# Two chains of moments in one slot of a transformer kernel's first phase, merged into one

## The reference

```python
x = x + attn_a(layernorm(x))   # 16 heads of 8, rotary, full softmax over 256 keys
x = x + ffn(layernorm(x))      # token shift, sigmoid(xr W_r) * (relu(xk W_k)^2 W_v)
x = x + attn_b(layernorm(x))   # windowed attention, one gradient step of a small MLP, gates
x = x + ffn(layernorm(x))
```

```python
def _layernorm(x, axis=-1, eps=1e-05):
    m = jnp.mean(x, axis=axis, keepdims=True)
    v = jnp.var(x, axis=axis, keepdims=True)
    return (x - m) / jnp.sqrt(v + eps)
```

## Time and profile before

| | us |
|---|---|
| median of 3 runs | 1386.79 |
| profiled execution, time | 1383.6 |
| profiled execution, span of the trace | 1381.8 |

### The profile page before, as it was taken

The page is one execution under the profiler, slowest core; times in us unless marked ns, Lnnn a source line. Parts: engine busy times, 40 slices in busy tenths (PEclk is TensorE's granted clock), DMA queues, the critical chain, the costliest instruction groups (busy, mean ns, idle before and its releaser), DMA issues.

```text
span 1381.8 us, 33016 instructions
## 1 busy us (share of the span) xinstructions
PE 1302.5 (94%) x10579; PEld 859.7 (62%) x10579; DVE 1125.4 (81%) x2849; ACT 904.5 (65%) x2504; POOL 503.6 (36%) x815
## 2 busy tenths in 40 slices
PE   6889999999999999987899999999999998999996
PEld 5445555555555555544566666666666665888885
DVE  5888988888999988875788888888888875787876
ACT  3268888888888888875456556655665653656563
POOL 5536666666666666532111111111111100233232
PEclk9999999999999999999999999999999999999998
DMA  3323322222233322210100110010000001223230
GB/s 79 78 74 80 83 77 75 68 80 80 80 90 102 102 74 79 64 42 16 32 24 28 32 49 26 26 32 24 28 28 29 20 17 42 77 81 89 81 87 29
DMA packets 101964, 79.62 MB, mean 58 GB/s; under 512 B 13780, under 2 KB 95124, under 8 KB 101796
## 3 DMA queue, kind: packets, MB, share of 16 engines
q1 hardware_dynamic: 100820, 76.99, 20.2%
q10 hardware_dynamic: 976, 0.54, 0.2%
HBM read 49.70 MB, written 27.79 MB: 56 GB/s over the span
## 4 chain that ended last, share of the span: by engine, by line
PE 49%; DVE 1%; issue 1%; ACT 0%; POOL 0%; DMA 0%; POOLq 0%; SPq 0%; DVEq 0%; ACTq 0%
PE b_g L1383 4%; PE b_psZ L1399 4%; PE b_psD L1320 4%; PE b_g L1370 4%; PE b_psZ L1331 4%; PE d_psO L1939 4%; PE d_psH L1931 4%; PE b_psM L1432 2%; PE b_psR L1376 2%; PE b_psL L1361 2%; PE b_psR L1392 2%; PE b_psD L1422 2%; PE b_psM L1444 1%; PE b_psM L1452 1%; PE d_psG L1957 1%
## 5 line engine op out<-in xcount | busy, mean ns | idle before, releaser
L793 DVE TENSOR_REDUCE a_MX<-a_psS 128x4 f32<-128x1024 f32 x248 | 302.7, 1220 | 40.2 <-PE a_psS L304 40.2
L596 ACT ACTIVATE a_PT<-a_psE 128x512 f32<-128x512 f32 x504 | 274.2, 603 | 56.8 <-PE a_psE L321 56.4
L1796 POOL TENSOR_TENSOR b_SWB<-b_b2col,b_SW 128x128 f32<-128x128 f32 x65 | 39.5, 608 | 367.3 <-ACT b_SW L1515 367.3
L335 PE MATMUL a_psV<-a_PT,a_VX 128*32 128x256 f32 x2048 | 138.8, 389 | 0.5 <-ACT a_PT L596 0.5
L1534 ACT ACTIVATE b_TH<-b_psZ 128x512 f32<-128x512 f32 x65 | 38.8, 597 | 128.8 <-PE b_psZ L1331 124.4
L304 PE MATMUL a_psS<-a_KS,a_QS 48*128 48x256 f16 x992 | 97.9, 275 | 20.4 <-DVE a_MX L793 15.9
L321 PE MATMUL a_psE<-a_QS,a_KS 50*128 50x256 bf16 x1008 | 98.0, 271 | 5.6 <-ACT a_PT L596 5.6
L1554 ACT ACTIVATE b_PR<-b_psL,b_mx 128x128 f32<-128x128 f32 x260 | 92.9, 368 | 6.4 <-DVE b_mx L1689 5.5
L335 PEld LDWEIGHTS a_psV<-a_PT,a_VX 128*32 128x32 f32 x2048 | 53.8, 110 | 52.4 <-issue 29.8
L304 PEld LDWEIGHTS a_psS<-a_KS,a_QS 48*128 48x128 bf16 x992 | 29.2, 94 | 89.5 <-DVE a_MX L793 57.1
L1682 DVE SCALAR_TENSOR_TENSOR b_HH<-b_TH,b_psZ 128x512 f32<-128x512 f32 x65 | 44.7, 687 | 43.5 <-ACT b_TH L1534 43.5
(11 more groups left out here) (300 smaller groups left out, 3392.5 us busy)
## 6 DMA issues: line engine op xcount, KB each, us to landing
a_KS<-kparts SPq DMA_DIRECT2D x63, 192.0 KB
a_QS<-qparts SPq DMA_DIRECT2D x126, 96.0 KB
qparts<-a_QP SPq DMA_DIRECT2D x64, 96.0 KB, 2.2
a_X<-x_in SPq DMA_DIRECT2D x32, 128.0 KB, 2.4
kparts<-a_KP SPq DMA_DIRECT2D x64, 64.0 KB, 2.1
x<-a_X SPq DMA_DIRECT2D x32, 128.0 KB, 1.8
b_X<-x SPq DMA_DIRECT2D x32, 128.0 KB, 2.9
zT<-b_XT SPq DMA_DIRECT2D x32, 128.0 KB, 1.7
```

What stands on the lines that cost most here:

```text
L335: mm = nc.tensor.matmul(psV[32 * h:32 * h + 32, 0:T], VX[:, b % UV, kt, at:at + 32], PT[:, gg, kt, h, :], start=(gg == 0 and kt == 0), sto ...
L596: nc.scalar.activation(PT[:, g % 2, :, h + s, :], shifted_bank(b, p, s), ACT.Exp).then_inc(S["exp"], 1)
L793: nc.vector.reduce_max(MX[:, b % 2, :].rearrange("q (s n) -> q s n", s=2)[:, :, 2 * p:2 * p + 2], score_banks(b, p)[:], AX.X).then_inc(S[" ...
```

## The change

A new function `both_moments(c)` takes the place of `stats(c + 1)` and `fstats(c - 6)` in slot 1 of VectorE's steps. It issues the statistics of both (four `bn_stats`), then the waits and one memset, then the four `bn_aggr`, then the affine operations: two of the input, one of the feed-forward input. The waits for X1 (`x1`) and for the last FZ (`fz`) now stand ahead of the input's aggregations. Where only one of the two is due, its chain is as before. `stats`, still used in the opening, and `fstats`, used in the closing, keep their sequence. Nothing else is changed, on no other engine.

```diff
+        def both_moments(c):
+            b, i = c + 1, c - 6
+            if on(b):
+                wait_dma(dve, x_in, b)
+                wait(dve, "z", b - 1)
+                wait(dve, "rr", b - 1)
+                for t in range(NT):
+                    nc.vector.bn_stats(st6[:, t, :], X[:, b % UX, t, :]).then_inc(S["stats"], 1)
+            if on(i):
+                wait(dve, "x1", i)
+                wait(dve, "fz", i - 1)
+                for t in range(NT):
+                    nc.vector.bn_stats(fst6[:, t, :], X1[:, i % 2, t, :]).then_inc(S["fstats"], 1)
+            if on(b):
+                wait(dve, "stats", b, per=2 * NT, done=NT)
+            if on(i):
+                wait(dve, "fstats", i, per=2 * NT, done=NT)
+            if on(b) or on(i):
+                nc.vector.memset(idle[:], 0.0)
+            if on(b):
+                for t in range(NT):
+                    nc.vector.bn_aggr(mv[:, t, :], st6[:, t, :]).then_inc(S["stats"], 1)
+            if on(i):
+                for t in range(NT):
+                    nc.vector.bn_aggr(fmv[:, t, :], fst6[:, t, :]).then_inc(S["fstats"], 1)
+            if on(b):
+                wait(dve, "stats", b, per=2 * NT)
+                affine(b)
+            if on(i):
+                wait(dve, "fstats", i, per=2 * NT)
+                nc.vector.tensor_scalar(fs[:], fmv[:, :, 1], EPS, None, ALU.add).then_inc(S["faffine"], 1)
+
...
@@ -919,8 +954,7 @@
                 if p == 1:
-                    if on(c + 1):
-                        stats(c + 1)
+                    both_moments(c)
...
-                if p == 1:
-                    if on(c - 6):
-                        fstats(c - 6)
```

More of the change, by code:

```diff
@@ L808, in stats, with affine @@
             moments(b, "stats", X[:, b % UX, :, :], st6, mv)
+            affine(b)
+        def affine(b):
             nc.vector.tensor_scalar(s12[:, 0, :], mv[:, :, 1], EPS, None, ALU.add).then_inc(S["affine"], 1)
```

## The result

The changed kernel takes 1395.83 us (median of 4 runs), the kernel before 1386.74 (median of 4 runs: one of them took 2120.62 us, the other three 1386.58 to 1386.79). The ratio on record, which leaves that one run out, is 1.0062, 95% interval 1.0043 to 1.008. The change makes the kernel 0.6 to 0.8% slower, well within 2%. The span of the profiled execution goes from 1381.8 to 1390.9 us.

The account below looks back on a forecast made before the run. The loop through GpSimd's start, FZ, TensorE and ScalarE was taken to bound full steps; 0.45 us more in each of 25 adds 11.2 us to 1386.8, giving 1398.0. Own range 1394 to 1402, widened down to 1387.

Parts of the forecast that it names:

- The loop and its link: Full steps: the loop runs through GpSimd's power, FZ, TensorE and ScalarE; GpSimd holds FZ's weight load by 0.05 us.
- The merged chain: VectorE, slot 1: the chain gets 0.31 us shorter per step, the input's second affine operation comes 0.49 us later.
- The cost in the loop: FZ's transpose, copy L667, ZT and ON's transpose each come 0.45 us later, making the step 18.7 us.
- A wrong term beside the loop: TensorE's slot 4 scores follow two transpose loads taking 0.24 us; VectorE's slot 4 loses only about 0.05 us.
- The sum: 25 full steps times 0.45 us make 11.2 us, 1398.0 us in all, + 0.8%.
- Whole durations: Foreign operations delay L810 by their durations, 0.86 us; kernel 20.5 us slower, about 1407; chance 0.04, including worse.
- Partly absorbed: TensorE or ScalarE catch up half the lateness: 5.6 us, 1392; chance 0.13, partly or wholly absorbed.
- The gain arrives: Slot 3's scores: 0.10 us per step gained, 1384.3, or all 0.31, 1379.0, if FZ has 0.49 us slack; chance 0.09.
- The merged waits stand still as before: VectorE gains only the memset, L810 comes 0.58 us later: 13.5 us, 1400.3; chance within the forecast's 0.74.

Follow-up runs that it names:

- e5: Changed kernel plus a 128 x 256 tile cleared on VectorE ahead of the input's affine operations: step 18.91 us, ratio to the kernel before 1.0151.
- e6: Changed kernel with GpSimd's power of the input statistics on four of six columns: step 18.37 us, ratio to the kernel before 1.002.
- e7: Kernel before, chains unmerged, feed-forward chain ahead of the input's on VectorE: 1417.42 us, ratio to the kernel before 1.0243.
- e2: Changed kernel with feed-forward power and FZ operations ahead of the input's power on GpSimd: step 18.21 us, ratio to the kernel before 1.0003.
- e8: Changed kernel, feed-forward aggregations and affine operation first on VectorE, feed-forward power and FZ first on GpSimd: 1383.17 us, ratio to before 0.9985.
- e1: Changed kernel with the input's two affine operations ahead of the feed-forward aggregations: step 18.69 us, ratio to the kernel before 1.0072.
- e4: Kernel before without one feed-forward statistic, one aggregation and the memset for most sequences on VectorE: step 18.20 us, ratio to the kernel before 0.9997.
- the medians of the second: Second comparison, more runs of the unaltered changed kernel against the kernel before: 1396.47 to 1384.0 us, ratio 1.0078.

## Why the prediction was right

*The loop and its link* held. FZ's weight load is 0.05 us behind GpSimd in both kernels, TensorE waits there in all 25 steps of the changed kernel, and from 5.58 us on moving FZ moved the step by as much, within 0.04 us (e5, e6, e7). Moving it further forward than 5.58 gave only 0.03 to 0.05 us (e2, e8). Changes to VectorE's length gave nothing (e1) or 0.04 us (e4).

*The merged chain.* Forecast: affine operation 0.49 later, VectorE 0.31 shorter. Measured: 0.48 and 0.33. The sum was right, two terms of it were not, and that they cancelled is luck. The third statistic starts 312.63 - 312.24 = 0.39 after the first, as I had it, but the first aggregation comes at 0.99, not 0.92; why VectorE stands still longer there is open. And the four aggregations and their successor follow each other faster than 0.09, so that L844 starts at 1.29 against 1.28 forecast. In e1 only the first slip acts, since no foreign aggregation stands ahead of the affine operations, and my forecast for it was wrong by 0.09 us.

*The cost in the loop.* Forecast + 0.45 us per step, measured 18.69 - 18.24 = 0.45. The copy L667 was forecast at 316.22 - 309.62 = 6.60 and is at 6.59; ZT at 8.99, measured 8.99; the transpose of ON at 9.51, measured 320.61 - 311.10 = 9.51. In front of the copy two slips of 0.03 to 0.04 us cancelled as well: the transpose of FZ was to start 0.03 after its load, at 315.77 - 309.62 = 6.15, and starts with it, at 317.21 - 311.10 = 6.11; the copy was to follow by 0.45 and follows by 317.69 - 317.21 = 0.48.

*A wrong term beside the loop.* The scores of slot 4 were to follow the transposes' first load by 0.24 us. They follow by 317.58 - 317.21 = 0.37, so slot 4's maximum is 0.14 us later instead of 0.05. It cost nothing, because the loop runs over ScalarE there.

*The sum.* Forecast 11.2 us and 1398.0; measured 9.1 in the first comparison, with 11.9 and 10.9 in the full steps of the two traces, and 12.5 between the medians of the second. The missing term is not in the loop but in the executions: the opening takes 105 to 113 us from one to the next in the traces of this study, so single runs of one kernel spread over 5 us.

*The rivals.* Whole durations (1407): the statistics' starts are 0.20 apart and the step grew by 0.45, not 0.82. The Trainium skill's rule, VectorE: DVE Perf Modes, "The DRAIN you can't avoid", that the next operation does not start until the pipe is empty, is not what these rows show: the operations start closer together than they last, after the change too. I had left out that the same section adds that a next operation that isn't held starts earlier, so the trace contradicts my reading of the rule more than the section. Partly absorbed: no. The gain arrives: it does where FZ has its 0.49 us of slack, as the condition said, and then 0.03 to 0.05 us of the 0.33 arrive (e2, e8). The merged waits stand still as before: no. Ahead of the affine operations the wait is gone (L844 starts about 0.07 us after the last aggregation, against 0.18), and ahead of the aggregations VectorE stands still once instead of twice, though about 0.08 us longer than it did in one chain. The Trainium skill's other rule, Perfetto Trace Analysis, "Optimizing Scalar/DVE Operations", that breaking work up may let it complete sooner where an engine that is not saturated causes bubbles on others, points the right way here. But e7, which merges nothing and loses more, shows that what counts is what stands ahead of the awaited result, merged or not.

## What to carry to other kernels

When an engine's work is batched to save its waits, ask for each result in the batch who waits for it and from when: here 0.33 us saved on an engine that waited later anyway cost 0.48 us on the one result that started a 3.3 us chain elsewhere. Find the loop that closes on itself, and measure its tightest link by a step in which the link is slack. A merge and the order of the queue that consumes it belong together: either alone was a loss, both together were none.

## What the runs showed of the hardware

*An instruction of VectorE was held by GpSimd.* L880 (L845 in the kernel before), one operation of the Newton iteration with which VectorE takes a reciprocal square root, takes 0.22 us by itself. In e2, whose Z is late, it overlaps GpSimd's addition L1086 (VectorE's and GpSimd's timelines, slot 1's maximum at 307.13):

```profile
313.90 1.21 DVE L793 TENSOR_REDUCE a_MX<-a_psS 128x4 f32<-128x1024 f32 x1
315.03 0.70 DVE L880 SCALAR_TENSOR_TENSOR a_psB<-a_hn 128x64 f32<-128x64 f32 x1
...
316.02 0.23 DVE L876 TENSOR_TENSOR a_psB<-a_hr,a_psB 128x64 f32<-128x64 f32 x1
316.16 1.22 DVE L793 TENSOR_REDUCE a_MX<-a_psS 128x4 f32<-128x1024 f32 x1
```

```profile
314.92 0.72 POOL L1086 TENSOR_TENSOR a_FX<-a_FC,a_FP 128x256 f32<-128x256 f32 x1
...
315.84 0.72 POOL L1086 TENSOR_TENSOR a_FX<-a_FC,a_FP 128x256 f32<-128x256 f32 x1 [0.20 <-ACT a_FP L668]
```

It takes 0.70 us and ends at 315.73, 0.09 us after GpSimd's addition has ended at 315.64. In the changed kernel the same operation takes 0.39 and ends 0.09 after that addition; its median is 0.32 us in e6 and 0.56 in e8. Both of its inputs are the same SBUF tile. L876, which reads one input from SBUF and one from PSUM, takes its usual 0.23 us in the middle of GpSimd's next addition. The Trainium skill, GPSIMD Engine Reference, "1. Specifications", names contention with VectorE instructions that have two SBUF inputs; the trace agrees. With what follows it, it makes slot 5's maximum 0.35 us later in e2 than before, but that costs the step next to nothing. In the median of e2's 25 steps this maximum ends at 10.26 us and slot 6's scores start at 10.31, 1.31 after the transpose of ON, instead of 1.28 as before and in e8. So the hold is worth 0.02 to 0.03 us of e2's step.

*With more waiting the clock dropped more often.* In a trace of the changed kernel one full step of 25 had it (stretches ahead of it and of the step itself):

```profile
330.00:404.00 74.00, 69.51 (x700) 41.33 (x700) 65.71 (x154) 61.68 (x147) 46.92 (x76) 1.00 0.29 78
404.60:424.30 19.70, 18.87 (x179) 10.93 (x177) 16.59 (x38) 15.63 (x38) 11.83 (x20) 0.91 0.32 83
```

That step took 19.77 us instead of 18.69. With FZ written 0.22 us later there were 5 such steps (e5), with 0.42 us later 11 (e7). Each of these counts is from one or two traces, but the mean clock of all runs goes the same way: 0.986 to 0.990 in the ten of the changed kernel, 0.981 to 0.986 in e5's four, 0.971 to 0.975 in e7's four. So in e5 and e7 TensorE's longer wait cost more than its own length; from what length on that is so these runs don't say.
